# Attention of a gated block: attended context copied by ScalarE and multiplied by W1, with the bias added to x by Pool

## Chip, cores and metric

The kernel runs on one core of one Trainium2 chip. The metric is the device time of one execution in microseconds, here the median of three runs. Below, TensorE is PE, VectorE is DVE, ScalarE is ACT, and Pool is the GpSimd engine.

## What is computed

The input x has 4 batches of 1024 tokens with 256 features, the context 4 batches of 154 tokens. The reference, cut to what matters:

```python
h = layernorm(x)
Sim = (h @ w1)[:, :, None] + (c @ w2)[:, None, :] + einsum('bid,bjd->bij', h * w3, c) + b_sim
A = softmax(Sim, axis=2)
hq_hat = einsum('bij,bjd->bid', A, c)                    # attended context
Batt = softmax(max(Sim, axis=2), axis=1)
hc_hat = broadcast(einsum('bi,bid->bd', Batt, h))        # one row per batch
feats = concat([h, hq_hat, h * hq_hat, h * hc_hat])
x = x + tanh(g_xattn) * (feats @ W_qv + b_qv)
y = layernorm(x)
x = x + tanh(g_ffn) * ffn(y)     # gated, with 16-bit quantized activations and 4-bit weights
```

W_qv has four blocks of 256 rows, W0 to W3. W1 is the block that multiplies the attended context.

## The kernel before

The kernel has two stages. The first, up to about 216 us of the profiled execution, does the attention, the residual and the second layer norm; the second is the feed-forward part. Only the first is touched.

The first stage works on 16 units n of 256 tokens, four per batch, in one software-pipelined loop over steps m, written out by hand once for each engine (N = 16, NP = 4, LAG = 7; b, s = m // 4, m % 4). There is no planner: every engine runs its list in order, and semaphores tie the lists together. In step m:

- PE (L615 to L654): `project(m-7)`, `turn_h(m)` (transposes of the normed x), `score(m-1)`, `turn_a(m-2)` (transposes of the softmax), `attend(m-3)` (L499, weights of the softmax times context, into hq_bank), `turn_y(m-8)`. In steps with s = 3 the projection stands at the end instead ("late"), so that two projections follow each other: project(0) and project(1), project(4) and project(5), and so on. In steps with s = 2 the projection has row sums of the batch between its matmuls and waits first for an exponent (eb_rdy) of ScalarE.
- ACT (L855 on): `turned_h(m)`, `norm_x(m+1)`, `batch_exp` in steps with s = 1, `turned_a(m-2)`, `exps(m-1)`, `normed(m-1)` (scales the softmax, waits for DVE's reciprocal), `turned_y(m-8)`, `context_k`, and the weight conversion `weight_f`.
- DVE (L1207 on): `context_bias`, `residual(m-7)` (x + tanh(g) times the projection, and its statistics), `scored(m-1)`, `row_shift`, `batch_max`, `norm_x1(m-7)` (second layer norm, waits for Pool's power), `normed(m-1)` (the reciprocal, L1046), `attended(m-3)` (L1048, the product of hq_bank with hT), `max_y`, `stats(m+3)`, and in some steps work on the feed-forward weights: `weight_scales` in steps 8, 12, 16, `weight_unit` in 10, 14, 18, `weight_values` in 11, 15, 19.
- Pool (L401 on): `y_std(m-7)` and `row_std(m+3)`, powers of two elements; `weight_q` in steps 9, 10, 13, 14, 17, 18 and `weight_n` in 11, 15, 19. `row_std` ends with step 12.

For one unit, `project` (L510) sums into PSUM: the transposed softmax aT times cw, the product prT times W2, and hT times we, where we joins W0 and W3. The tile cw is the context times W1 plus the bias: PE multiplies it once per batch (`context_w`, L457, in step 1 and in every step with s = 0), and DVE adds the bias and stores it (`context_wv`, L1024, one step later). Two places wait for it: the first projection of a batch, and `batch_max` on PE (L562), which writes the same PSUM bank m_bank and waits with

```python
pe.wait_ge(cw_rdy, min(b + 2, B))
```

`attend(n)` writes hq_bank and waits for pr_rdy, that is for DVE's product of the unit before.

## Time and profile before

| | |
|---|---|
| median of 3 runs | 488.28 us (487.01 to 489.61) |
| profiled execution: time | 486.99 us |
| profiled execution: span | 485.2 us |
| mean granted clock of TensorE | 0.993 of full speed |
| PE busy | 461.5 us (95%) |
| DVE busy | 344.0 us (71%) |
| ACT busy | 266.7 us (55%) |
| Pool busy | 63.1 us (13%) |

The span reaches from the first to the last instruction of the core; the execution's own time has 1.8 us around it. Busy shares are means over both stages. The granted clock is what the chip allows TensorE at a time, as a share of 2.4 GHz; 0.50 is 1.2 GHz. A line number such as L1054 is a line of the kernel before; a number in brackets at the end of a timeline row is the idle time of that engine before the instruction, with what ended it.

### The profile page before, as it was taken

Reading aid. Unit: us, or ns where it says so; the run is one execution under the profiler, and the core shown is the slowest. Engines: PE = TensorE matmul, PEld = TensorE weight load, DVE = VectorE, ACT = ScalarE, POOL = GpSimd, SP = SyncE. Lnnn points to the kernel's source line nnn. Section 1 sums busy time; section 2 is a strip of 40 time slices with the busy share of each in tenths; the row PEclk is TensorE's granted clock in tenths of the full one; section 3 lists DMA queues with packets and bytes.
Section 4 is the critical chain, followed back from the end, with each engine's and each line's share of the span. In section 5 each row is a group of like instructions: output and inputs, shape, how many; then the busy total and the mean of one; then the engine's idle time right before and its main releaser. Section 6 shows DMA issues by size and latency. Waiting matters only on the chain.

```text
span 485.2 us, 6854 instructions
## 1 busy us (share of the span) xinstructions
PE 461.5 (95%) x2528; PEld 304.6 (63%) x2528; DVE 344.0 (71%) x649; ACT 266.7 (55%) x325; POOL 63.1 (13%) x61
## 2 busy tenths in 40 slices
PE   4899999998999997998999999999999999799997
PEld 3787884986578846783444444444444444588886
DVE  6455483859264935687644378999998888898874
ACT  3795142624241300426633459999567777888760
POOL 1111111213110311310000003343200000000000
PEclk9999999999899998999999999999999999999999
DMA  8930000200020002002000000000000000234442
GB/s 236 327 119 1 0 2 0 88 0 1 1 88 0 1 0 86 2 0 88 0 0 0 0 1 0 0 1 0 0 1 1 0 0 0 88 111 151 135 142 72
DMA packets 20673, 21.15 MB, mean 44 GB/s; under 512 B 825, under 2 KB 20392, under 8 KB 20648
## 3 DMA queue, kind: packets, MB, share of 16 engines
q1 hardware_dynamic: 20628, 20.82, 13.5%
q8 instruction: 15, 0.25, 0.2%
q14 instruction: 10, 0.08, 0.1%
q10 hardware_dynamic: 20, 0.00, 0.0%
HBM read 12.43 MB, written 8.39 MB: 43 GB/s over the span
## 4 chain that ended last, share of the span: by engine, by line
PE 68%; issue 15%; DVE 13%; ACT 2%; POOL 1%; DMA 1%; ACTq 0%; POOLq 0%; DVEq 0%
PE ps L676 17%; PE ps L711 11%; PE ps L681 9%; PE ps L527 4%; PE ps L506 4%; PE ps L531 4%; PE ps L523 4%; PE ps L569 3%; PE ps L486 3%; PE ps L472 1%; PE ps L495 1%; DVE st L1066 1%; PE ps L462 1%; DVE xa L1062 1%; DVE yb L1079 1%
## 5 line engine op out<-in xcount | busy, mean ns | idle before, releaser
L676 PE MATMUL ps<-xh,wuh 128*128 128x512 f16 x192 | 72.8, 379 | 0.1
L676 PE MATMUL ps<-xh,wul 128*128 128x512 f16 x192 | 72.8, 379 | 0.0
L681 PE MATMUL ps<-xl,wuh 128*128 128x512 f16 x192 | 57.1, 379 | 0.0
L1300 DVE TENSOR_REDUCE cols<-hid x10 | 22.9, 2286 | 24.7 <-ACT hid L891 24.7
L711 PE MATMUL ps<-wdl,oh 128*128 128x256 f16 x168 | 37.4, 273 | 0.0
L711 PE MATMUL ps<-wdh,oh 128*128 128x256 f16 x168 | 37.4, 273 | 0.0
L676 PE MATMUL ps<-xh,wgh 128*128 128x512 f16 x96 | 36.4, 379 | 0.7 <-DVE xh L1288 0.7
L676 PE MATMUL ps<-xh,wgl 128*128 128x512 f16 x96 | 36.4, 379 | 0.0
L527 PE MATMUL ps<-wv,prT 128*128 128x256 f32 x128 | 35.9, 396 | 0.0
L523 PE MATMUL ps<-cw,aT 77*128 77x256 f32 x128 | 34.7, 385 | 0.9 <-ACT cols L840 0.9
L783 ACT ACTIVATE hT<-ps 128x512 f32<-128x512 f32 x16 | 9.5, 591 | 46.6 <-PE ps L472 46.6
L531 PE MATMUL ps<-we,hT 128*128 128x256 f32 x128 | 34.4, 392 | 0.0
L891 ACT ACTIVATE hid<-ps 128x2048 f32 x10 | 18.8, 1875 | 27.9 <-PE ps L681 27.9
L676 PEld LDWEIGHTS ps<-xh,wuh 128*128 (+1 forms) x192 | 18.8, 98 | 23.1 <-issue 0.6
L681 PEld LDWEIGHTS ps<-xl,wuh 128*128 (+1 forms) x192 | 18.8, 98 | 22.7
L676 PEld LDWEIGHTS ps<-xh,wul 128*128 (+1 forms) x192 | 18.8, 98 | 22.5
L506 PE MATMUL ps<-aT,cx 77*128 77x256 f32 x128 | 31.2, 388 | 0.0
L1360 DVE TENSOR_TENSOR gq<-gq,ps 128x2048 bf16<-128x2048 int16 x11 | 25.1, 2285 | 6.0 <-ACT au L943 6.0
L973 ACT ACTIVATE oq<-hid,cols 128x1536 int16 (+1 forms) x15 | 23.6, 1571 | 10.2 <-DVE ol L1416 10.2
L1321 DVE TENSOR_REDUCE cols<-ps 128x1 f32<-128x2048 f32 x12 | 27.4, 2287 | 2.1 <-PE ps L681 2.1
L527 PEld LDWEIGHTS ps<-wv,prT 128*128 128x128 f32 x128 | 23.6, 192 | 8.2 <-issue 5.2
L681 PE MATMUL ps<-xl,wgh 128*128 128x512 f16 x96 | 28.6, 379 | 0.0
(211 smaller groups left out, 953.5 us busy)
## 6 DMA issues: line engine op xcount, KB each, us to landing
x_scratch<-xa SPq DMA_DIRECT2D x4, 1024.0 KB, 4.4
xo<-x_scratch SPq DMA_DIRECT2D x16, 256.0 KB, 2.7
out_dram<-xo SPq DMA_DIRECT2D x15, 256.0 KB, 2.1
xa<-in_x SPq DMA_DIRECT2D x3, 1024.0 KB, 12.6
xa<-in_x SPq DMA_DIRECT2D x4, 256.0 KB, 4.3
wv<-in_L_xattn_W_qv SPq DMA_DIRECT2D x1, 1024.0 KB, 8.6
wr<-in_L_ffn_w_gate SPq DMA_DIRECT2D x1, 768.0 KB, 9.5
wr<-in_L_ffn_w_up SPq DMA_DIRECT2D x1, 768.0 KB, 10.9
```

Of the source, the lines that this page charges most:

```text
L506: mm = pe.matmul(hq_bank[:, d * PT:(d + 1) * PT], cx[b][0:JP, k, d * P:(d + 1) * P], aT[0:JP, par, k, q], start=k == 0, stop=k == 1)
L523: pe.matmul(o_, aT[0:JP, par, k, q], cw[0:JP, b % 3, k, :], start=k == 0, stop=False)
L527: pe.matmul(o_, prT[:, par, d, q], wv[:, 2 * KD + d, :], start=False, stop=False)
L531: mm = pe.matmul(o_, hT[:, par, d, q], we[:, par, d, :], start=False, stop=d == KD - 1)
L676: pe.matmul(ps[hf][:, q, :], w_[:, d, ds(k * P, P)], xh[:, d, n], start=d == 0 and w_ is wh, stop=False)
L681: mm = pe.matmul(ps[hf][:, q, :], wh[:, d, ds(k * P, P)], xl[:, d, n], start=False, stop=d == KD - 1)
L711: mm = pe.matmul(down_ps(par)[:, t], o_[:, par, k, q], w_[:, k, :], start=not low and k == 0 and w_ is wdh, stop=low and k == KF - 1)
L891: act.activation(unit(hid, k, hf), ps_half(hf), ACT.Copy).then_inc(half_free[hf], 1)
L973: act.activation(oq[:, par], hid[:, :, ds(c * CD, CD)], ACT.Copy, scale=c_co).then_inc(oqa_rdy, 1)
L1300: dve.tensor_reduce(gmx[:, ds(k * 2 + hf, 1)], unit(hid, k, hf), AX.X, ALU.max, apply_absolute_value=True).then_inc(gm_done, 1)
L1321: dve.tensor_reduce(umx[:, u:u + 1], ps_half(u % 2), AX.X, ALU.max, apply_absolute_value=True).then_inc(half_free[u % 2], 1)
L1360: dve.tensor_tensor(g_.bitcast(BF16), g_, ps_half(hf), ALU.mult).then_inc(half_free[hf], 1)
```

## The change

PE no longer multiplies the context by W1. ScalarE copies the attended context of every unit from hq_bank to SBUF (hqT), and the projection takes hqT times W1 in place of aT times cw. DVE's product reads hqT instead of hq_bank. The bias, multiplied by tanh(g), is added to x by Pool (`bias_x`), and the residual waits for it. aT shrinks to a ring of three units.

```diff
--- before.py
+++ after.py
@@ -144,7 +144,7 @@
     a = copy_of(r_hid)
     xa = place(a, "xa", [P, B * TB, D], F32)
     hT = place(a, "hT", [P, 2, KD, S], F32)
-    aT = place(a, "aT", [JP, 2, 2, S], F32)
+    hqT = place(a, "hqT", [P, 2, KD, S], F32)
     prT = place(a, "prT", [P, 2, KD, S], F32)
     h = place(a, "h", [P, 2, TB, D], F32)
 
@@ -156,7 +156,7 @@
     cx01 = place(a, "cx01", [JP, 2, 2, D], F32)
     cx23 = place(copy_of(r_wg), "cx23", [JP, 2, 2, D], F32)
     cx = [cx01[:, 0], cx01[:, 1], cx23[:, 0], cx23[:, 1]]
-    cw = place(a, "cw", [JP, 3, 2, D], F32)
+    aT = place(a, "aT", [JP, 3, 2, PT], F32)
 
     a = copy_of(r_wd)
     cbi = place(a, "cbi", [P, 2, J], F32)
...
@@ -395,6 +395,14 @@
                 wm = wr[:, m, :].rearrange("p (n k) -> p n k", k=QB)
                 pool.tensor_tensor(wm, wm, wsc[:].unsqueeze(2).broadcast_to([P, NB, QB]), ALU.mult).then_inc(wn_rdy, 1)
 
+            def bias_x(n):
+
+                pool.wait_ge(h_rdy, n + 1)
+                if n == 0:
+                    pool.wait_ge(txb_rdy, 1)
+                x_ = xa[:, 2 * n:2 * n + 2, :]
+                pool.tensor_tensor(x_, x_, txb[:].unsqueeze(1).broadcast_to([P, 2, D]), ALU.add).then_inc(xb_rdy, 1)
+
             pool.wait_ge(mhalf_rdy, 1)
             for n in range(NP):
                 row_std(n)
@@ -403,6 +411,8 @@
                     y_std(m - LAG)
                 if 1 <= m and m + 3 < N:
                     row_std(m + 3)
+                if 4 <= m < N + 4:
+                    bias_x(m - 4)
                 for i in range(3):
                     if m in (W_AT[i] - 1, W_AT[i]):
                         weight_q(i, m - W_AT[i] + 1)
@@ -441,7 +451,7 @@
             def turn_context(b):
                 pe.wait_ge(cx_in[b], 16)
                 ge(pe, hc_rdy, b - 1)
-                ge(pe, cw_rdy, b)
+                ge(pe, cbi_rdy, b)
                 for k in range(2):
                     for d in range(KD):
                         tr = pe.transpose(m_bank[:, d * J + k * JP:d * J + (k + 1) * JP],
@@ -453,15 +463,6 @@
                 for d in range(KD):
                     mm = pe.matmul(m_bank[:, 0:J], w2b[:, d, :], cxT[:, d, :], start=(d == 0), stop=(d == KD - 1))
                 mm.then_inc(cbi_ps, 1)
-
-            def context_w(b):
-                pe.wait_ge(cbi_rdy, b + 1)
-                pe.wait_ge(wqv_in, 16)
-                for k in range(2):
-                    for d in range(KD):
-                        mm = pe.matmul(m_bank[0:JP, k * D:(k + 1) * D], cxT[:, d, k * JP:(k + 1) * JP], wv[:, KD + d, :],
-                                       start=(d == 0), stop=(d == KD - 1))
-                mm.then_inc(cw_ps, 1)
 
             def turn_h(n):
                 b, s, par = place_of(n)
@@ -499,12 +500,11 @@
             def attend(n):
                 b, s, par = place_of(n)
                 pe.wait_ge(aT_rdy, n + 1)
-                ge(pe, pr_rdy, n)
-                q = slice(s * PT, (s + 1) * PT)
+                ge(pe, hqT_rdy, n)
                 for d in range(KD):
                     for k in range(2):
                         mm = pe.matmul(hq_bank[:, d * PT:(d + 1) * PT], cx[b][0:JP, k, d * P:(d + 1) * P],
-                                       aT[0:JP, par, k, q], start=k == 0, stop=k == 1)
+                                       aT[0:JP, n % 3, k, :], start=k == 0, stop=k == 1)
                 mm.then_inc(hq_ps, 1)
 
             def project(n, summed=None):
@@ -512,17 +512,18 @@
                 if summed is not None:
                     pe.wait_ge(eb_rdy, summed + 1)
                 pe.wait_ge(pr_rdy, n + 1)
+                if n == 0:
+                    pe.wait_ge(wqv_in, 16)
                 if s == 0:
-                    pe.wait_ge(cw_rdy, b + 1)
                     pe.wait_ge(we_rdy, b + 1)
                 ge(pe, x1_rdy, n - 1)
                 for t in range(2):
                     q = slice(s * PT + t * P, s * PT + (t + 1) * P)
                     o_ = last_f(t) if n == L else f_bank[n % 2][:, t * D:(t + 1) * D]
-                    for k in range(2):
-                        pe.matmul(o_, aT[0:JP, par, k, q], cw[0:JP, b % 3, k, :], start=k == 0, stop=False)
+                    for d in range(KD):
+                        pe.matmul(o_, hqT[:, par, d, q], wv[:, KD + d, :], start=d == 0, stop=False)
                         if summed is not None:
-                            row_sum(summed, 4 * t + k)
+                            row_sum(summed, 4 * t + d)
                     for d in range(KD):
                         pe.matmul(o_, prT[:, par, d, q], wv[:, 2 * KD + d, :], start=False, stop=False)
                         if summed is not None:
@@ -561,7 +562,7 @@
 
             def batch_max(b):
                 pe.wait_ge(diag_rdy, b + 1)
-                pe.wait_ge(cw_rdy, min(b + 2, B))
+                pe.wait_ge(cbi_rdy, min(b + 2, B))
                 pe.matmul(m_bank[:, 0:P], ones[:], diag[:], start=True, stop=True).then_inc(m_ps, 1)
 
             def row_sum(b, t):
@@ -645,10 +646,6 @@
                     turn_y(m - LAG - 1)
                 if s == 3 and b + 1 < B:
                     context_bias(b + 1)
-                if m == 1:
-                    context_w(0)
-                if s == 0 and 1 <= b < B:
-                    context_w(b)
                 if LAG <= m and late:
                     project(m - LAG)
                 if N + 3 <= m < N + 6:
@@ -803,9 +800,16 @@
             def turned_a(n):
                 b, s, par = place_of(n)
                 act.wait_ge(at_ps, n + 1)
+                ge(act, hq_ps, n - 2)
+                act.activation(aT[0:JP, n % 3, :, :],
+                               a_bank[0:JP, :].rearrange("p (k n) -> p k n", k=2), ACT.Copy).then_inc(aT_rdy, 1)
+
+            def attended(n):
+                b, s, par = place_of(n)
+                act.wait_ge(hq_ps, n + 1)
                 ge(act, f_ps, n - 2 * NP + 1)
-                act.activation(aT[0:JP, par, :, s * PT:(s + 1) * PT],
-                               a_bank[0:JP, :].rearrange("p (k n) -> p k n", k=2), ACT.Copy).then_inc(aT_rdy, 1)
+                act.activation(hqT[:, par, :, s * PT:(s + 1) * PT], hq_bank.rearrange("p (d n) -> p d n", d=KD),
+                               ACT.Copy).then_inc(hqT_rdy, 1)
 
             def turned_y(n):
                 act.wait_ge(yT_ps, n + 1)
@@ -822,7 +826,7 @@
 
             def turned_context(b):
                 act.wait_ge(cxT_ps, b + 1)
-                ge(act, cw_ps, b)
+                ge(act, cbi_ps, b)
                 act.activation(cxT[:], m_bank[:, 0:2 * J].rearrange("p (d j) -> p d j", d=KD), ACT.Copy).then_inc(cxT_rdy, 1)
 
             def context_k(b):
@@ -869,6 +873,8 @@
                     normed(m - 1)
                 if s == 1 and b == 1:
                     batch_exp(b - 1)
+                if 3 <= m <= N + 2:
+                    attended(m - 3)
                 if LAG < m:
                     turned_y(m - LAG - 1)
                 if s == 3 and b + 1 < B:
@@ -1021,12 +1027,6 @@
                 dve.wait_ge(cbi_ps, b + 1)
                 dve.tensor_scalar(cbi[:, b % 2, :], m_bank[:, 0:J], c_bs, None, ALU.add).then_inc(cbi_rdy, 1)
 
-            def context_wv(b):
-                dve.wait_ge(cw_ps, b + 1)
-                ge(dve, f_ps, NP * (b - 2))
-                dve.tensor_tensor(cw[0:JP, b % 3], m_bank[0:JP, :].rearrange("p (k n) -> p k n", k=2),
-                                  bqb[0:JP, :].unsqueeze(1).broadcast_to([JP, 2, D]), ALU.add).then_inc(cw_rdy, 1)
-
             def scored(n):
                 b, s, par = place_of(n)
                 dve.wait_ge(sc_ps, n + 1)
@@ -1048,16 +1048,16 @@
             def attended(n):
                 b, s, par = place_of(n)
                 q = slice(s * PT, (s + 1) * PT)
-                dve.wait_ge(hq_ps, n + 1)
+                dve.wait_ge(hqT_rdy, n + 1)
                 dve.wait_ge(hT_rdy, n + 1)
                 ge(dve, f_ps, n - 2 * NP + 1)
-                dve.tensor_tensor(prT[:, par, :, q], hq_bank.rearrange("p (d n) -> p d n", d=KD), hT[:, par, :, q],
-                                  ALU.mult).then_inc(pr_rdy, 1)
+                dve.tensor_tensor(prT[:, par, :, q], hqT[:, par, :, q], hT[:, par, :, q], ALU.mult).then_inc(pr_rdy, 1)
 
             def residual(n):
 
                 g = 2 * n
                 dve.wait_ge(f_ps, n + 1)
+                dve.wait_ge(xb_rdy, n + 1)
                 x_ = xa[:, g:g + 2, :]
                 dve.scalar_tensor_tensor(x_, f_bank[n % 2].rearrange("p (t d) -> p t d", t=2), c_tx, x_,
                                          ALU.mult, ALU.add).then_inc(x1_rdy, 1)
@@ -1082,6 +1082,7 @@
 
             def last_y():
 
+                dve.wait_ge(xb_rdy, N)
                 for t in range(2):
                     x_ = xa[:, 2 * L + t, :]
                     dve.wait_ge(l_f_ps, t + 1)
@@ -1128,6 +1129,8 @@
                 dve.tensor_scalar(c_hc, m_bank[:, HC:HC + KD], c_rs, None, ALU.mult).then_inc(hc_rdy, 1)
                 dve.wait_ge(hc_rdy, b + 1)
                 ge(dve, f_ps, NP * (b - 1))
+                if b == 0:
+                    dve.wait_ge(wqv_in, 16)
                 for d in range(KD):
                     i_ = dve.scalar_tensor_tensor(we[:, b % 2, d, :], wv[:, 3 * KD + d, :], c_hc[:, d:d + 1], wv[:, d, :],
                                                   ALU.mult, ALU.add)
@@ -1198,21 +1201,16 @@
             dve.wait_ge(x0_in[2], 16)
             stats(2)
             row_shift(1)
-            dve.tensor_copy(bqb[:], f_bank[1][:, 0:D]).then_inc(bqb_rdy, 1)
             dve.wait_ge(x0_in[3], 16)
             stats(3)
             row_shift(2)
-            dve.wait_ge(bqb_rdy, 1)
             dve.wait_ge(tanh_rdy, 1)
+            dve.tensor_scalar(txb[:], f_bank[1][:, 0:D], c_tx, None, ALU.mult).then_inc(txb_rdy, 1)
             for m in range(N + LAG - 1):
                 b, s = m // NP, m % NP
                 late = s == 3
                 if m == 0:
                     row_shift(3)
-                if m == 2:
-                    context_wv(0)
-                if s == 1 and 1 <= b < B:
-                    context_wv(b)
                 if s == 0 and 1 <= b < B:
                     context_bias(b)
                 if s == 2 and 1 < b <= B:
```

On DVE, steps 12 and 13, from the product of unit 9 to the residual of unit 6. Before:

```order
L1054 TENSOR_TENSOR prT<-ps,hT 128x2x256
L1106 TENSOR_REDUCE cols<-yb 128x1
L1004 BN_STATS st<-xa 128x6 x2
L1007 BN_AGGR cols<-st 128x2 x2
L1011 TENSOR_SCALAR cols<-cols 128x2
L1146 TENSOR_REDUCE wsc<-wr 128x48
L1148 TENSOR_SCALAR wsc<-wsc 128x48
L1149 TENSOR_REDUCE cols<-wsc 128x1
L1150 TENSOR_SCALAR wdiag<-ident,cols 128x128
L1151 RECIPROCAL wri<-wsc 128x48
L1027 TENSOR_TENSOR cw<-ps,bqb 77x512
L1062 SCALAR_TENSOR_TENSOR xa<-ps,cols,xa 128x512
```

And with the change:

```order
L1054 TENSOR_TENSOR prT<-hqT,hT 128x2x256
L1107 TENSOR_REDUCE cols<-yb 128x1
L1010 BN_STATS st<-xa 128x6 x2
L1013 BN_AGGR cols<-st 128x2 x2
L1017 TENSOR_SCALAR cols<-cols 128x2
L1149 TENSOR_REDUCE wsc<-wr 128x48
L1151 TENSOR_SCALAR wsc<-wsc 128x48
L1152 TENSOR_REDUCE cols<-wsc 128x1
L1153 TENSOR_SCALAR wdiag<-ident,cols 128x128
L1154 RECIPROCAL wri<-wsc 128x48
L1062 SCALAR_TENSOR_TENSOR xa<-ps,cols,xa 128x512
```

The addition that made cw has gone, and the product reads hqT (SBUF) instead of PSUM; the order is otherwise the same.

On ACT, from turned_a to context_k in step 11, with the change (before, the row of hqT isn't there):

```order
L804 ACTIVATE aT<-ps 77x512
L788 ACTIVATE sc,cols<-sc,cols 128x154 x2
L797 ACTIVATE sc<-sc,cols 128x154 x2
L811 ACTIVATE hqT<-ps 128x2x256
L816 ACTIVATE yT<-ps 128x2x256
L836 ACTIVATE cp<-cxT,wcol 128x154 x2
```

The copy to hqT stands behind the exponentials and the scaling (L797) of a unit two later.

On Pool, from y_std(5) in step 12 to weight_n in step 15, with the change (L377 is y_std, L373 row_std, L404 bias_x, L390 and L396 weight_q and weight_n):

```order
L377 TENSOR_TENSOR cols<-cols 128x2
L373 TENSOR_TENSOR cols<-cols 128x2
L404 TENSOR_TENSOR xa<-xa,txb 128x512
L377 TENSOR_TENSOR cols<-cols 128x2
L404 TENSOR_TENSOR xa<-xa,txb 128x512
L390 TENSOR_TENSOR wr<-wr,wri 128x768
L377 TENSOR_TENSOR cols<-cols 128x2
L404 TENSOR_TENSOR xa<-xa,txb 128x512
L390 TENSOR_TENSOR wr<-wr,wri 128x768
L377 TENSOR_TENSOR cols<-cols 128x2
L404 TENSOR_TENSOR xa<-xa,txb 128x512
L396 TENSOR_TENSOR wr<-wr,wsc 128x1536
```

In step 12 bias_x stands behind row_std; from step 13 on it stands directly behind y_std and ahead of the weight instruction.

## Rows read from the trace of the kernel before

**Rows 1.** Busy us by stretch: PE, PEld, DVE, ACT, POOL, then PEclk, DMA share, GB/s.
```profile
24.00:36.00 12.00, 12.00 (x74) 10.52 (x73) 7.01 (x34) 11.05 (x33) 1.88 (x3) 1.00 0.37 128
...
108.00:120.00 12.00, 9.95 (x53) 8.22 (x52) 11.65 (x31) 4.94 (x12) 4.15 (x3) 1.00 0.00 1
```
**Rows 2.** Groups by line, first stage: busy us, mean ns | idle before.
```profile
L1106 DVE TENSOR_REDUCE cols<-yb 128x1 f32<-128x512 f32 x15 | 10.2, 679 | 0.2
L783 ACT ACTIVATE hT<-ps 128x512 f32<-128x512 f32 x16 | 9.5, 591 | 46.6 <-PE ps L472 46.6
```
**Rows 3.** Timeline, steps 12 to 14: start us, duration us, engine, line, operation.
```profile
113.35 0.67 DVE L1054 TENSOR_TENSOR prT<-ps,hT 128x512 f32<-128x512 f32 x1
...
114.11 0.57 ACT L812 ACTIVATE yT<-ps 128x512 f32<-128x512 f32 x1
...
118.48 0.62 DVE L1027 TENSOR_TENSOR cw<-ps,bqb 77x512 f32<-77x512 f32 x1
119.02 0.73 DVE L1062 SCALAR_TENSOR_TENSOR xa<-ps,cols,xa 128x512 f32<-128x512 f32 x1
119.25 0.46 PE L565 MATMUL ps<-diag,ones 128*128 128x128 f32 x2 [2.06 <-DVE cw L1027]
...
120.94 0.28 DVE L1118 TENSOR_REDUCE cols<-ps 128x1 f32<-128x128 f32 x1
...
125.31 0.60 PE L523 MATMUL ps<-cw,aT 77*128 77x256 f32 x2
```
**Rows 4.** Timeline, from the batch reduction of step 17 to project(11).
```profile
169.00 0.28 DVE L1118 TENSOR_REDUCE cols<-ps 128x1 f32<-128x128 f32 x1
...
169.76 0.70 PE L523 MATMUL ps<-cw,aT 77*128 77x256 f32 x2 [0.92 <-ACT cols L840]
```
**Rows 5.** Stretches of 1 us behind two waits; PEclk is third from the end.
```profile
121.00:122.00 1.00, 1.00 (x6) 0.99 (x5) 0.39 (x3) 1.00 (x4) 0.89 (x2) 0.50 0.00 0
...
189.00:190.00 1.00, 1.00 (x4) 0.82 (x3) 0.00 (x0) 0.00 (x0) 0.00 (x0) 0.50 0.00 0
```
**Rows 6.** Timeline, three other waits of TensorE (steps 15, 19 and 20).
```profile
143.97 0.66 PE L495 MATMUL ps<-ident,sc 128*77 128x128 f32 x4 [0.79 <-ACT sc L800]
...
187.28 0.66 PE L542 MATMUL ps<-ident,yb 128*128 128x128 f32 x4 [2.97 <-DVE yb L1079]
...
202.87 1.76 PE L600 MATMUL ps<-ident,wr 128*128 128x128 f32 x12 [1.13 <-DVE wgl L1172]
```
**Rows 7.** Timeline of TensorE: context_w(2) in step 8, then step 9 to project(3).
```profile
63.15 1.89 PE L462 MATMUL ps<-wv,cxT 128*77 128x256 f32 x8
...
64.88 1.03 PE L523 MATMUL ps<-cw,aT 77*128 77x256 f32 x4
...
70.06 0.39 PE L565 MATMUL ps<-diag,ones 128*128 128x128 f32 x2
...
74.38 0.60 PE L523 MATMUL ps<-cw,aT 77*128 77x256 f32 x2
```
**Rows 8.** Timeline of the start: the first exponent and the first row sums.
```profile
35.96 0.28 ACT L840 ACTIVATE cols<-cols 128x8 f32<-128x8 f32 x1
...
37.26 3.62 PE L569 MATMUL ps<-h,cols 128*1 128x256 f32 x16
```
**Rows 9.** Timeline, Pool and VectorE side by side in steps 16 and 17; last, all of L1079: min/median/max ns.
```profile
158.76 2.77 POOL L396 TENSOR_TENSOR wr<-wr,wsc 128x1536 f32<-128x1536 f32 x1 [3.95 <-ACT wr L844]
...
159.06 2.50 DVE L1073 TENSOR_SCALAR cols<-cols 128x2 f32<-128x2 f32 x1
...
169.16 0.69 POOL L377 TENSOR_TENSOR cols<-cols 128x2 f32<-128x2 f32 x1 [6.84 <-DVE cols L1073]
...
169.81 1.48 POOL L390 TENSOR_TENSOR wr<-wr,wri 128x768 f32<-128x768 f32 x1
169.89 1.88 DVE L1079 TENSOR_SCALAR yb<-xa,cols 128x256 f32<-128x256 f32 x2 [0.61 <-POOL cols L377]
...
L1079 DVE TENSOR_SCALAR yb<-xa,cols x30: 400/408/1554, 56.9 to 213.0; 128x256 f32<-128x256 f32 x30
```

More of the change, by code:

```diff
@@ L167, in build @@
     wrow = place(a, "wrow", [3 * KD, P], F32)
-    bqb = place(a, "bqb", [P, D], F32)
+    txb = place(a, "txb", [P, D], F32)
     hrow = place(copy_of(r_wu), "hrow", [1, D], F32)
```

8 lines of the change are left out of this document (4 added, 4 removed).

## The prediction, made before the changed kernel was run

> **What bounds the kernel now.** I read the stretches first [rows 1]. The change lies in the first stage, up to about 216 us. In the start ScalarE is nearly full (11.05 of 12 us). Later TensorE is busy nearly all the time; where it falls short (9.95 of 12 us from 108 to 120), VectorE is at 11.65. So TensorE sets the pace in most steps and VectorE in a few. The groups by line give durations [rows 2]; then I read the timeline at the gaps.
>
> Step m means pass m of the main loop; n is a unit of 256 tokens, projected at step n+7. Where two projections stand back to back, VectorE catches up. In steps 12/13 and 16/17 it doesn't: behind the product it runs weight_scales, the residual and the batch maximum, and the next projection with row sums waits for all of it through ScalarE's exponent. At step 13 TensorE waits 2.06 us at L565 for cw, which VectorE built just before [rows 3]; before project(11) it waits 0.92 us for the exponent [rows 4].
>
> **TensorE's clock.** After the 2.06 us wait the granted clock goes to 0.50, that is 1.2 instead of 2.4 GHz, and it does so after the 2.97 us wait at 187.28 [rows 5, 6]. The waits of 0.92 and 0.79 us are followed by no such stretch. The price: from L565 to the projection the same work takes 74.38 − 70.06 = 4.32 us at step 9 [rows 7] and 125.31 − 119.25 = 6.06 us at step 13 [rows 3], so 1.74 us for a fall.
>
> **What is removed.** context_w runs four times.
> - Step 8: 64.88 − 63.15 = 1.73 us of TensorE [rows 7], taken whole: TensorE then reaches project(3) at 74.38 − 1.73 = 72.65, and VectorE, which loses context_wv there and gains the wait described below, has the exponent ready at about 72.7. **−1.73**.
> - Step 12: the same 1.73 us, the 2.06 us wait, and its fall of the clock, 1.74: 5.53 us. TensorE would reach project(7) at 125.31 − 5.53 = 119.78 [rows 3]. What is late next is the exponent, see below.
> - Steps 1 and 4 lie in the start, under ScalarE's work; without that cover they would bring 1.7 us each.
>
> **What is added: a handover.** ScalarE copies the attended context: 16 copies at 0.59 us [rows 2], 9.5 us in all. By itself that costs little, since ScalarE is mostly idle after step 7. What counts is the place. VectorE's product of unit m−3 now needs a copy that stands in ScalarE's queue behind normed(m−1), which itself waits for the reciprocal directly in front of that product. At step 12 the product started at 113.35. ScalarE is through with normed at 114.11, where turned_y starts; the copy takes 0.59, the hop 0.05: 114.75, **1.40 us later** [rows 3]. Behind it on VectorE stand max_y, the statistics, weight_scales. Where TensorE has 10 us of projections ahead, this is hidden; where VectorE sets the pace, it is not.
> - Step 12/13: the residual comes at 119.02 + 1.40 − 0.54 (context_wv gone, start to start) = 119.88. To the batch reduction it is 120.94 − 119.02 = 1.92 us [rows 3], from there to TensorE's restart 0.76 [rows 4]: 122.6. TensorE is there at 119.78 and waits 2.8 us. I take a new fall of the clock, since 2.06 us was enough: it gains 125.31 − 122.6 − 1.74, **−1.0**. So of 5.5 us removed one is left.
> - Step 16/17: the same 1.40 us, with no context_wv to set against it: **+1.40**.
> - Start, steps 3 to 5: exponentials, normed, copy, product, statistics and scores now form one ring over two engines. Copy and product together add up to 1.2 us a step, 3.6 in three; against that go a ScalarE wait behind context_w(0), 0.5 us, the slack of either engine, and the exponent's head start on the row sums (35.96 against 37.26) [rows 8]. Bounds −0.5 (the slack takes all) and +1.5; I take **+0.15**, near the lower, as both engines still wait in every one of these steps now.
>
> **What is added: the bias on Pool.** 16 adds of 512 elements. Pool takes 2.77 us for 1536 elements and 1.48 for 768 [rows 9]: 1.69 ns an element, 1.05 us for 512 (ends: 0.69 for its two-element instruction, 1.48 for 768). They are ready three steps before the residual. What isn't covered is who is kept out: beside Pool's L396 a two-element TENSOR_SCALAR of VectorE takes 2.50 us, and norm_x1 (L1079) takes 1.88 beside L390 [rows 9], where 0.73 is usual for two of about 0.41. From step 13 on Pool has no row_std, so bias_x follows y_std at once, and norm_x1 waits for the same y_std. Pool's next instruction starts 0.65 us after y_std, VectorE's 0.73; VectorE is let go some 0.15 us before Pool's end (159.06 + 2.50 − 0.17 against 158.76 + 2.77): 0.65 + 1.05 − 0.15 − 0.73 = 0.8, taken as **0.75 us a meeting**.
> - Steps 15 and 16, norm_x1(8) and (9), both on the way to the exponent before project(11): **+1.5**. With the handover that wait is 0.92 + 1.40 + 1.5 = 3.8 us, so the clock falls: **+1.74**.
> - Step 14: bias_x(10) pushes weight_q behind it, and both keep out L1132 and the small instructions after it, on the way to turn_a(13), which waits 0.79 us already [rows 6]. Between +0.3 (VectorE gets in between the two) and +1.25 (it doesn't): **+0.7**.
> - Step 18, the same before the 2.97 us wait, with L1132 starting ahead of Pool: bounds +0.2 and +1.2, **+0.4**.
> - Step 19: norm_x1(12) delays the weight values and so turn_w(1), which waits 1.13 us already [rows 6]: **+0.75**.
>
> The Trainium skill's "GPSIMD Engine Reference" (section "Elementwise — side-by-side cycle accounting") has a two-input add at 1.96 times VectorE's; on this trace's 0.67 us for the product that is an estimate of 1.3 us. By it each meeting costs 0.3 us more and the sum 0.9 more; no run here shows it yet.
>
> The product now reads two SBUF tensors instead of one and PSUM. VectorE's 512-element reduction from SBUF takes 0.679 us [rows 2], the product from PSUM 0.67 [rows 3]: no difference taken. The Trainium skill's "VectorE: DVE Perf Modes" (section on the TRN2 errata) charges PSUM 62 cycles more, an estimate of 0.06 us; by it steps 12 and 16 would each get that back. The projection's matmuls keep their 256 columns, so I take nothing for them.
>
> **Sum.** −1.73 − 1.0 + 1.40 + 0.15 + 1.5 + 1.74 + 0.7 + 0.4 + 0.75 = +3.9 us. On the profiled execution's 486.99 that is 490.9. The median of the runs, 488.28, lies 1.3 above it, so I predict **492.2**.
>
> **Rivals.** About 0.5% (2.4 us) is what a measurement of this kernel can tell from no change.
> - *The clock stays up and Pool's adds slip past* (faster). For it: 0.92 us cost no clock, and Pool's and VectorE's starts are only 0.08 us apart, so VectorE may come first. Then −1.73 − 2.7 + 1.40 + 0.15 = −2.9: **485.4**. It decides before project(7) and project(11): waits of 2.8 and 2.3 us must leave the clock at 1.00. Against it: 2.06 us didn't. Chance 0.15.
> - *Handover only*: Pool's adds miss VectorE, the clock falls twice. −1.73 − 1.0 + 1.40 + 1.74 + 0.15 = +0.6: **488.9**. Chance 0.24.
> - *Pool's queue becomes the bound*: weight_q takes its place right behind bias_x in steps 14 and 18 (+0.55, +0.8), and the wait before turn_a(13) grows to 2 us, so the clock falls there too (+1.74): **495.3**. Chance 0.14.
> - The forecast, itself 490 to 494: 0.47.
>
> **Numbers.** Range 486.0 to 495.5: all but the better part of the first rival and the tail of the third, under 2 in 10 together. Slower by over 0.5% (above 490.7), most of the forecast and the third: 0.54. Faster (below 485.8): 0.14. The same: 0.32.
>
> **What would show it.** A product 1.3 to 1.5 us after its reciprocal in steps 12 and 16; 1.4 to 1.6 us for the two norm_x1 instructions from step 13 on, beside a Pool instruction of 1.05 us; TensorE waiting 2.8 us before project(7) and 3.8 before project(11), each followed by a stretch at 0.50; no wait at L565. It is wrong if TensorE's wait before project(11) stays under 2 us, if norm_x1 keeps its 0.73, or if Pool's add takes much more than 1.5 us.

## The result, and the profile after

| | before | changed |
|---|---|---|
| median | 488.94 us | 499.04 us |
| range | 487.01 to 490.62 (4 runs) | 495.89 to 500.75 (4 runs) |
| profiled execution | 486.99 us | 498.97 us |
| its span | 485.2 us | 497.1 us |
| mean granted clock | 0.993 | 0.976 |

The change makes the kernel slower: 1.020 times the time of before, with a 95% interval of 1.016 to 1.024, some 10 us. I had forecast 492.2, with 486.0 to 495.5 as the range. The sign was right, the size was not.

The head of the page of the changed kernel, and then the shares of its chain that ended last:

```profile
PE 462.5 (93%) x2496; PEld 302.4 (61%) x2496; DVE 352.9 (71%) x645; ACT 274.6 (55%) x341; POOL 81.6 (16%) x77
...
PE   4789999997989697898999999999999999899997
...
PEclk9999999999899887989999999999999999899999
...
PE 50%; DVE 20%; issue 19%; ACT 8%; POOL 1%; DMA 0%; ACTq 0%; POOLq 0%; DVEq 0%
```

TensorE has about as much busy time as before (462.5 us against 461.5), though context_w is gone and 32 matmuls with it. So the busy time is not what the 12 us of the span are made of in any simple way: part of the work simply ran at a lower clock. The clock's row has five 8s and one 7 (a slice is 12.4 us); three of these lie side by side, from 161 to 199 us. On the chain TensorE has 50%, before it had 68%. That row prices nothing by itself: in e3 below, which is faster than before, it is 46%.

The four large waits of TensorE in the first stage, and the one before turn_a(13), from the timeline of the changed kernel (start us, us, engine, line, operation, tiles, and in brackets the idle time before and who ended it):

```profile
122.52 0.70 PE L524 MATMUL ps<-wv,hqT 128*128 128x256 f32 x2 [3.03 <-ACT cols L844]
...
143.86 0.66 PE L496 MATMUL ps<-ident,sc 128*77 128x128 f32 x4 [0.96 <-ACT sc L797]
...
173.27 1.22 PE L524 MATMUL ps<-wv,hqT 128*128 128x256 f32 x2 [4.09 <-ACT cols L844]
...
193.19 1.11 PE L543 MATMUL ps<-ident,yb 128*128 128x128 f32 x4 [3.23 <-DVE yb L1079]
...
210.65 1.86 PE L601 MATMUL ps<-ident,wr 128*128 128x128 f32 x12 [2.08 <-DVE wgl L1175]
```

The first stands where before had 2.06 us at the batch maximum [rows 3]. The third is the 0.92 us before project(11) [rows 4], now 4.09. The others are those of [rows 6]: 0.79, 2.97 and 1.13 us, now 0.96, 3.23 and 2.08. And what the clock did around them (stretch, its length, busy us and count of PE, PEld, DVE, ACT, POOL, then the granted clock, DMA share, GB/s):

```profile
120.00:122.00 2.00, 0.00 (x0) 0.00 (x0) 1.90 (x9) 0.00 (x0) 0.07 (x1) 1.00 0.00 0
122.00:127.00 5.00, 4.48 (x10) 1.47 (x10) 3.68 (x10) 3.08 (x11) 3.35 (x3) 0.66 0.01 2
171.00:173.00 2.00, 0.00 (x0) 0.00 (x0) 1.68 (x7) 0.18 (x1) 0.33 (x1) 0.55 0.00 0
173.00:178.00 5.00, 4.73 (x9) 1.67 (x10) 4.03 (x4) 1.66 (x5) 3.09 (x3) 0.50 0.02 3
...
191.00:193.00 2.00, 0.00 (x0) 0.00 (x0) 1.86 (x7) 0.00 (x0) 1.33 (x1) 0.67 0.21 70
193.00:198.00 5.00, 4.80 (x14) 3.96 (x15) 1.34 (x3) 0.60 (x1) 0.00 (x0) 0.50 0.00 2
210.00:212.00 2.00, 1.35 (x10) 1.09 (x11) 2.00 (x4) 1.93 (x5) 2.00 (x1) 1.00 0.00 0
212.00:216.00 4.00, 4.00 (x14) 3.29 (x13) 3.05 (x10) 1.04 (x2) 0.85 (x2) 0.57 0.02 4
430.00:435.00 5.00, 5.00 (x33) 3.77 (x32) 3.80 (x6) 5.00 (x5) 0.00 (x0) 0.66 0.27 94
```

A stretch's length times (1 − clock) is the clock lost in it. 122 to 127 lost 5 × 0.34 = 1.7 us, 212 to 216 and 430 to 435 the same. 171 to 178 lost 0.9 + 2.5 = 3.4, twice as much in one piece, and 191 to 199 again 3.4. Over the whole span the mean clock gives the total: 0.024 × 497.1 = 11.9 us, against 0.007 × 485.2 = 3.4 before. I call 1.7 us of lost clock **one fall**; before had two, the changed kernel has seven. What was lost inside the wait itself can cost nothing, since TensorE did nothing there: up to the two restarts that is 1.0 us of the third place (from 171.2 to 173.27) and 0.8 of the fourth.

These counts are of the two profiled executions. By their mean clocks the four runs of the changed kernel lost 8.4 to 13.5 us, about five to eight falls; the 26 runs of before that stand beside e1 lost about one to three (0.996 to 0.989).

The same landmarks of TensorE in the two timelines give a ledger. The forecast's column adds up its own terms in their order.

| reached by TensorE | before | changed | shift | forecast |
|---|---|---|---|---|
| turn_h in step 8 | 59.05 | 60.22 | +1.17 | +0.15 |
| turn_h in step 9 | 70.28 | 69.72 | −0.56 | −1.58 |
| turn_a(13) | 143.97 | 143.86 | −0.11 | −1.88 |
| project(11) | 169.76 | 173.27 | +3.51 | +1.02 |
| turn_y(11) | 187.28 | 193.19 | +5.91 | +3.16 |
| turn_w(1) | 202.87 | 210.65 | +7.78 | +3.91 |
| first matmul of stage two | 225.24 | 234.70 | +9.46 | +3.91 |
| end of the span | 485.2 | 497.1 | +11.9 | +3.9 |

### The profile page after: what moved, and what is told of

Its sections match the earlier page's. It is cut to its first block, busy times and chain, and to the rows that moved or that the text cites. A ratio compares the mean times of both kernels' runs of the same rounds, so it can differ in the third digit from the quotient of the medians.

```text
span 497.1 us, 6840 instructions
## 1 busy us (share of the span) xinstructions
PE 462.5 (93%) x2496; PEld 302.4 (61%) x2496; DVE 352.9 (71%) x645; ACT 274.6 (55%) x341; POOL 81.6 (16%) x77
## 3 DMA queue, kind: packets, MB, share of 16 engines
q1 hardware_dynamic: 20628, 20.82, 13.3%
## 4 chain that ended last, share of the span: by engine, by line
PE 50%; DVE 20%; issue 19%; ACT 8%; POOL 1%; DMA 0%; ACTq 0%; POOLq 0%; DVEq 0%
PE ps L708 11%; PE ps L673 8%; PE ps L524 5%; PE ps L528 4%; PE ps L678 4%; DVE cols L1319 4%; PE ps L532 4%; PE ps L570 4%; PE ps L506 3%; DVE hid L1335 2%; PE ps L487 2%; ACT hid L920 2%; DVE yb L1079 1%; DVE st L1066 1%; DVE xa L1062 1%
## 5 line engine op out<-in xcount | busy, mean ns | idle before, releaser
L524 PE MATMUL ps<-wv,hqT 128*128 128x256 f32 x128 | 38.1, 415 | 7.1 <-ACT cols L844 7.1
L528 PE MATMUL ps<-wv,prT 128*128 128x256 f32 x128 | 37.4, 410 | 0.0
L524 PEld LDWEIGHTS ps<-wv,hqT 128*128 128x128 f32 x128 | 24.5, 204 | 13.5 <-ACT cols L844 7.6
L528 PEld LDWEIGHTS ps<-wv,prT 128*128 128x128 f32 x128 | 24.9, 202 | 9.3 <-issue 6.1
L1335 DVE CUSTOM_DVE_ANT_0 hid<-ag,sq 128x2048 f32<-128x2048 int16 x12 | 29.1, 2424 | 0.2
## 6 DMA issues: line engine op xcount, KB each, us to landing
xa<-in_x SPq DMA_DIRECT2D x3, 1024.0 KB, 12.4
```

Source lines behind the costliest of these rows:

```text
L524: pe.matmul(o_, hqT[:, par, d, q], wv[:, KD + d, :], start=d == 0, stop=False)
L528: pe.matmul(o_, prT[:, par, d, q], wv[:, 2 * KD + d, :], start=False, stop=False)
L1335: dve.tensor_tensor_reduce(half_of(hid, u), ag[:, u % 2, :], sq[u % 2][:], 1.0, 0.0, ALU.mult, ALU.max, pmx[:, u:u + 1]).then_inc(p_rdy, 1)
```

## The experiments

Each kernel ran 4 to 10 times, beside runs of before on the same chip (medians 488.75 to 489.13 us). "Lost" is the clock lost in the profiled execution, added up over stretches of 1 us.

| | median us | ratio to before, 95% | lost us |
|---|---|---|---|
| changed kernel | 499.04 | 1.020 [1.016, 1.024] | 11.9 |
| bias later (e1) | 490.85 | 1.004 [1.000, 1.008] | 6.8 |
| product from PSUM (e2) | 492.58 | 1.008 [1.005, 1.010] | 10.2 |
| both (e3) | 485.77 | 0.995 [0.993, 0.998] | 3.4 |
| bias add left out (e8) | 491.63 | 1.005 [1.002, 1.008] | 6.8 |
| waits filled (e4) | 491.78 | 1.007 [1.004, 1.010] | 1.7 |
| one wait filled (e12) | 497.22 | 1.016 [1.013, 1.020] | 8.5 |
| before, waits filled (e7) | 486.12 | 0.995 [0.992, 0.997] | 1.7 |
| product last, bias later (e6) | 482.97 | 0.989 [0.985, 0.993] | 3.4 |
| e6, filled (e10) | 480.64 | 0.984 [0.981, 0.987] | 0.0 |
| e3, copy later, filled (e9) | 480.76 | 0.984 [0.981, 0.986] | 0.0 |

### The bias behind norm_x1

```
                 if 4 <= m < N + 4:
+                    if 13 <= m:
+                        pool.wait_ge(y_rdy, m - LAG + 1)
                     bias_x(m - 4)
```

> From step 13 on Pool's add waits until norm_x1 of the same step is done, so the two no longer meet. Theory A (handover, Pool's meetings and clock falls add up, a fall of 3.4 us behind a wait of over 3 us): the wait before project(11) goes from 4.09 to about 1.9 us, turn_w(1)'s from 2.08 to about 1.1; with the clock that comes back the time falls from 499.0 by 6 to 9 us, to 490 to 493. Theory B (the handover alone makes the loss, Pool's adds are incidental): 497 to 499. Theory C (Pool's queue is what matters, later adds push weight_q further): 499 or more.

Measured 490.85 us, 8.2 under the changed kernel, as expected. Two waits were not: I expected about 1.9 us before project(11) and 1.1 before turn_w(1). TensorE's waits in its timeline:

```profile
124.67 0.86 PE L526 MATMUL ps<-wv,hqT 128*128 128x256 f32 x2 [3.01 <-ACT cols L846]
...
144.37 0.66 PE L498 MATMUL ps<-ident,sc 128*77 128x128 f32 x4 [0.22 <-ACT sc L799]
...
172.29 0.70 PE L526 MATMUL ps<-wv,hqT 128*128 128x256 f32 x2 [2.92 <-ACT cols L846]
...
190.06 1.12 PE L545 MATMUL ps<-ident,yb 128*128 128x128 f32 x4 [1.73 <-DVE yb L1081]
...
206.15 1.76 PE L603 MATMUL ps<-ident,wr 128*128 128x128 f32 x12 [1.73 <-DVE wgl L1177]
```

The wait before project(7) stays at 3.0 us, so moving Pool's add does nothing there. Before project(11) it goes from 4.09 to 2.92, so the edit brings 1.2 us there; without any add (e8, below) the wait is 2.33, and what the other 0.6 is made of was not traced. Before turn_a(13) it goes to 0.22, less than before's 0.79 [rows 6], and before turn_y(11) to 1.73 against 2.97. The reason is weight_q, which stands behind the add and now starts later too. In before it runs beside VectorE's two instructions that make `we` for the next batch, in the changed kernel the add does and then weight_q, and in e1 neither. Step 14, of before, the changed kernel and e1:

```profile
139.91 1.46 DVE L1132 SCALAR_TENSOR_TENSOR we<-wv,cols 128x256 f32<-128x256 f32 x2
```

```profile
138.77 2.49 DVE L1135 SCALAR_TENSOR_TENSOR we<-wv,cols 128x256 f32<-128x256 f32 x2
```

```profile
140.89 0.88 DVE L1137 SCALAR_TENSOR_TENSOR we<-wv,cols 128x256 f32<-128x256 f32 x2
```

In step 18 the three take 2.13, 1.94 and 0.88 us. So part of e1's gain is a delay of weight_q, which has nothing to do with the bias. The rest of the 8.2 us is clock: three falls fewer in the profiled execution, 5.1 us.

### The product straight from PSUM

VectorE reads hq_bank as before the change, ScalarE copies when VectorE is done, and the projection waits for the copy.

```
-                dve.wait_ge(hqT_rdy, n + 1)
+                dve.wait_ge(hq_ps, n + 1)
...
-                dve.tensor_tensor(prT[:, par, :, q], hqT[:, par, :, q], hT[:, par, :, q], ALU.mult)
+                dve.tensor_tensor(prT[:, par, :, q], hq_bank.rearrange("p (d n) -> p d n", d=KD), hT[:, par, :, q], ALU.mult)
...
-                act.wait_ge(hq_ps, n + 1)
+                act.wait_ge(pr_rdy, n + 1)
...
-                pe.wait_ge(pr_rdy, n + 1)
+                pe.wait_ge(hqT_rdy, n + 1)
```

> VectorE's product reads PSUM again, as before, and ScalarE copies the attended context behind it; Pool's adds stay. Theory A: VectorE no longer waits 1.28 us for the copy; the waits before project(7) and project(11) shrink by 1.4 us each, to 1.6 and 2.7 us, and one or two quanta of clock (1.7 us each) come back: 492 to 495. Theory B (the handover makes the whole loss): 484 to 488, below the kernel before. Theory C (Pool makes the whole loss): 498 to 500.

Measured 492.58 us, 6.5 under the changed kernel.

```profile
118.87 0.70 PE L524 MATMUL ps<-wv,hqT 128*128 128x256 f32 x2 [1.62 <-ACT cols L844]
...
166.66 1.22 PE L524 MATMUL ps<-wv,hqT 128*128 128x256 f32 x2 [2.70 <-ACT cols L844]
...
189.06 1.09 PE L543 MATMUL ps<-ident,yb 128*128 128x128 f32 x4 [5.04 <-ACT yT L816]
```

Both waits for the exponent are 1.4 us shorter than in the changed kernel (3.03 to 1.62, 4.09 to 2.70): that is the handover as forecast, 1.40, at both places. The edit also made a wait of its own. ScalarE's copy at 187.83 stands in its queue ahead of turned_y and now waits for the product, which stands behind norm_x1 on VectorE; so TensorE waited 5.04 us for yT at 189.06. The clock lost 3.4 us around the 2.70 (166 to 173) and 3.4 around the 5.04 (186 to 194), 1.2 of it inside that wait.

### Both together

> Both edits together: product from PSUM with the copy behind it, and Pool's adds behind norm_x1. Theory A: what is left is the removal of context_w and context_wv against 16 copies and adds that nothing waits for; wait before project(7) about 1.6 us, before project(11) about 0.9, clock falls as in the kernel before or one fewer: 482 to 486, under the 488.9 of before. Rival (the matmuls on 128 rows, or the copies themselves, cost something in every step): 488 to 492.

Measured 485.77 us. With both costs out, the change's idea is a little faster than before: ratio 0.995 with an interval of 0.993 to 0.998. The waits are 1.63, 1.54, 3.53 (the new wait for yT) and 1.73 us, and only around the 3.53 was clock lost, 3.4 us. The two costs together are 13.3 us of time. Alone they bring 8.2 and 6.5, sum 14.7, so they are nearly independent. I had expected a wait of about 0.9 us before project(11); it was 1.54. And not all of the gain over before is the change's: in e3 too the two instructions for `we` take 0.88 us, where before has 1.46 and 2.13.

### No bias add at all

The kernel leaves out Pool's adds and the waits on them, so that the output lacks the bias.

> The changed kernel with the addition of the bias on Pool left out, so the output lacks the bias; the handover through ScalarE stays. Theory A: as with the later adds (490.9), and less, since weight_q and weight_n come 1.3 us earlier and L1135 is held once only: 488 to 491, with a wait before project(11) of about 2.3 us (0.92 + 1.40). Rival (even the later adds cost nothing): 490.5 to 491.5. If the handover were free: 484.

```profile
123.89 0.70 PE L522 MATMUL ps<-wv,hqT 128*128 128x256 f32 x2 [2.70 <-ACT cols L842]
...
171.53 0.70 PE L522 MATMUL ps<-wv,hqT 128*128 128x256 f32 x2 [2.33 <-ACT cols L842]
...
190.58 1.12 PE L541 MATMUL ps<-ident,yb 128*128 128x128 f32 x4 [2.98 <-DVE yb L1076]
...
205.92 1.76 PE L599 MATMUL ps<-ident,wr 128*128 128x128 f32 x12 [1.13 <-DVE wgl L1171]
```

Measured 491.63 us: the handover alone costs 2.5 us net of the gain of context_w. The wait before project(11) is 2.33 us, 0.01 from 0.92 + 1.40, and turn_y(11) and turn_w(1) wait as long as before (2.98 and 1.13). This is my second rival, "handover only", for which I had worked out 488.9. Its waits come out and its time is 2.7 us above it: there were four falls where that sum had three (1.7 us). The fourth came at 46 us, behind a wait of 0.98 us that the sum didn't have (see the start, below). And e8 is level with e1, so an add placed behind norm_x1 costs nothing that can be seen in the median: it lengthens two waits by 0.6 us each and shortens turn_y(11)'s by 1.25, by the delay of weight_q.

### Filling TensorE's waits

Matmuls whose result nobody reads (the projection that follows starts its sums anew over them) are put into the queue ahead of the waiting instruction: 6 before project(7), 9 before project(11), 7 before turn_y(11), 4 before turn_w(1), of 256 columns each. They only keep TensorE at work.

```
+            def fill(n, k):
+                pe.wait_ge(x1_rdy, n - 1)
+                for i in range(k):
+                    pe.matmul(f_bank[n % 2][:, 0:D], ident[:], wv[:, 0, :], start=True, stop=True)
...
+                if m in {14: 6, 18: 9}:
+                    fill(m - LAG, {14: 6, 18: 9}[m])
```

> The changed kernel with TensorE kept busy in its four long waits by matmuls that nobody reads: 6 before project(7), 9 before project(11), 7 before turn_y(11), 4 before turn_w(1). Nothing else moves. Theory A (the waits cost clock, 1.7 us of it for 2 to 3 us and 3.4 us for longer): the 10.2 us of clock lost in the first stage come back, except what the fillers overrun; 489 to 492, with the granted clock at 1.00 there. Rival (the low clock is there for another reason, or costs nothing since other engines set the pace): 497 to 500.

Measured 491.78 us, 7.3 under the changed kernel, with VectorE, ScalarE and Pool as they were there. The clock lost 1.7 us instead of 11.9, in one fall at 45 us that no filling matmul was near. That is what the waits' clock costs the changed kernel, not yet its share of the change's 10 us, since before loses clock in its waits as well.

The same was done to the kernel before, with 4 such matmuls ahead of the batch maximum of step 13 and 6 ahead of turn_y(11):

> The kernel before, with its two long waits filled by matmuls that nobody reads: 4 at the batch maximum of step 13 (2.06 us), 6 before turn_y(11) (2.97 us). Theory A: the clock no longer falls there and 2 x 1.7 us come back: 485.0 to 486.0 against 488.7. Rival (the fall at step 13 is hidden by VectorE, which sets the pace there): 486.5 to 487.5, only the second comes back. If neither counts: 488 to 489.

486.12 us, 3.0 under before, just above the 485.0 to 486.0 expected. Both falls of the first stage are gone, and one came at 415 us, in stage two. With the waits of both kernels filled, 491.78 stands against 486.12: 5.7 of the 10.1 us between the medians remain, and 4.4 are clock. By the spans (489.1 against 483.5) it is 5.6 and 6.3 of 11.9. Without its clock, before has a span of 485.2 − 3.4 = 481.8; this kernel's is 483.5 − 1.7 = 481.8. So the filling matmuls cost nothing that can be seen here.

Then the changed kernel with the 9 before project(11) alone:

> The changed kernel with fillers before project(11) only (9, in the wait of 4.09 us). Theory A (the clock lost behind this one wait is 3.4 us, and all of it is time): 495 to 496, with the granted clock at 1.00 from 171 to 179 us. If a fall costs 1.7 us however long the wait, as the prediction took it: 497 to 498. If nothing comes back: 499.

```profile
170.00:178.00 8.00, 7.79 (x35) 4.77 (x33) 7.17 (x15) 1.84 (x5) 3.42 (x3) 1.00 0.01 2
190.00:196.00 6.00, 3.59 (x11) 3.08 (x12) 3.42 (x10) 0.60 (x1) 1.54 (x1) 0.72 0.11 37
```

From 170 to 178 us the clock stays at 1.00, where the changed kernel was at 0.50. The median is 497.22, 1.8 us lower, and the span 1.8 lower. That is the time of the expectation's rival, in which a fall costs 1.7 us however long the wait. But behind that wait 2.4 us of clock had been lost. Two other places differ: a fall came at 45 to 50 us, which the changed kernel's profile doesn't have, after the same wait of 0.98; and behind turn_y(11)'s wait, 3.23 us in both, the clock lost 6 × 0.28 = 1.7 us instead of the 2.7 that lay behind it in the changed kernel. −2.4 + 1.7 − 1.0 = −1.7, near to the −1.8 measured. Whether filling one wait moved the other falls or they differ from execution to execution, this pair of profiles can't tell; the same wait of 0.98 us had a fall behind it in e1, e4, e8 and e11 too.

### What Pool's add costs

In one run the add's second operand was changed so that it stands still: each of 16 columns of the bias is added to 32 columns of x (the output has a wrong bias for it).

> The changed kernel with 16 columns of the bias tile, each repeated 32 times, added in place of all 256 twice, so the output has a wrong bias; Pool's add has as many elements as in the change, but its second operand stands still for 32 elements at a time, as in weight_q. If the estimate of the prediction failed because weight_q's second operand stands still (1.69 ns an element), the add takes about 1.05 us in place of 1.27. If two-input work on Pool costs the same whatever the operand: 1.27.

The group of Pool's adds, of the changed kernel and then of this one (count, busy us, mean ns, idle before):

```profile
L404 POOL TENSOR_TENSOR xa<-xa,txb 128x512 f32<-128x512 f32 x16 | 20.3, 1268 | 0.0
```

```profile
L404 POOL TENSOR_TENSOR xa<-xa,txb 128x512 f32<-128x512 f32 x16 | 16.8, 1047 | 0.0
```

With the standing operand it takes 1.047 us, and my 1.05 was right for that kind. I had read 1.69 ns an element from weight_q [rows 9], whose scale is one number for 32 elements, and carried it over to an add whose bias moves at every element. The single run took 497.81 us. The two instructions that the add held in steps 15 and 16 took 1.45 and 1.18 us, 0.2 less each, and the wait before project(11) went from 4.09 to 3.96.

### A better place for the product

If ScalarE's copy comes late, VectorE can do its other work first. In e6 VectorE's product stands at the end of the step, and the bias behind norm_x1:

```
-                if 3 <= m <= N + 2:
-                    attended(m - 3)
                 if LAG <= m and late:
                     residual(m - LAG)
...
                 if N + 3 <= m < N + 6:
                     weight_parts(m - N - 3)
+                if 3 <= m <= N + 2:
+                    attended(m - 3)
```

> Product from hqT as in the change, but as VectorE's last work of a step, behind the statistics and the weight work; Pool's adds behind norm_x1. Theory A: the copy is then always there in time, the 1.28 us waits of VectorE vanish, and the product itself (0.6 us) leaves the way to the exponent too: wait before project(7) about 1.0 us, before project(11) about 0.9; 483 to 486, as good as the product from PSUM or better. Rival (a product at the end delays the scores of the next step in the start and gives the gain back): 487 to 490.

482.97 us, 1.1% under before. VectorE's wait at the product goes from 18.3 us in 14 waits to 2.1 in all. TensorE's four waits are 1.73, 1.63, 1.73 and 1.72 us; I had expected about 1.0 and 0.9 for the first two. All three engines do the change's work, and the span without lost clock is 481.2 − 3.4 = 477.8, 4.0 under that of before. Not all of the 4.0 need be the change's. The waits before turn_a(13) and turn_y(11) are 0.22 and 1.73 us, 1.8 less together than in before, and in e1, which has the same two, this came from weight_q starting later. The kernel before with weight_q moved back, and nothing else, was not run, so how much of the gain it would reach alone is open.

Two kernels put the parts together. e10 is e6 with 2, 2, 5 and 3 filling matmuls:

> Product from hqT as VectorE's last work of a step, Pool's adds behind norm_x1 (483.0 without fillers, 3.4 us of clock lost in its profiled run, 1.7 of it in the first stage), with fillers: 2 before project(7), 2 before project(11), 5 before turn_y(11), 3 before turn_w(1). If the clock is the only thing fillers bring: 480.5 to 481.5, level with the 480.8 of the version that multiplies from PSUM. If the 5 fillers overrun the 1.73 us wait before turn_y(11): 482 to 483.

e9 is e3 with ScalarE's copy moved behind turned_y, so that yT is not late, and 3, 3, 5 and 3 of them:

> Product from PSUM, ScalarE's copy behind it and behind turned_y, Pool's adds behind norm_x1, and fillers: 3 before project(7), 3 before project(11), 5 before turn_y(11), 3 before turn_w(1). The version without fillers took 485.8 with 3.4 us of clock lost in the profiled run. Theory A: all of it comes back and turn_y(11) waits 1 to 1.5 us less: 481 to 483. Rival (the fillers overrun the waits and cost what they save): 485 to 486.

480.64 us, as expected, and 480.76, just below what was; both are 1.6% under before and level with each other. The clock's row of e10 shows no slice below 9, and from 119 us on (e9's timeline) TensorE's waits at the old places are under half a microsecond:

```profile
PEclk9999999999999999999999999999999999999999
```

```profile
119.82 0.70 PE L526 MATMUL ps<-wv,hqT 128*128 128x256 f32 x2 [0.36 <-ACT cols L858]
...
165.02 0.70 PE L526 MATMUL ps<-wv,hqT 128*128 128x256 f32 x2 [0.24 <-ACT cols L858]
...
196.00 1.76 PE L609 MATMUL ps<-ident,wr 128*128 128x128 f32 x12 [0.42 <-DVE wgl L1189]
```

## Why the prediction was wrong in size and right in sign

**The step that failed is the term of the clock**: "1.74 for a fall", taken at most once per wait, and with one added fall in the sum. The profiled execution has five more falls than before, not one. Of its 11.9 us of lost clock 1.8 lie inside waits; the 10.1 behind them, against 3.4 before, are 6.7 us more, where the sum had 1.74. That is 5.0 of the 8.0 us by which the span missed. The other 3.0 are mostly the start (1.0), stage two beside its fall (0.7), and 0.3 each in steps 9 to 12, in step 14 and before project(11). The price of one fall was right (1.71 measured); how many there would be was not. The median missed by 6.8: the 1.3 us that the sum put on top of the profiled execution was before's, and the changed kernel's median lies 0.1 above its own.
- Before project(11) I had a wait of 3.8 us and one fall. It was 4.09, the clock was already at 0.55 in the last 2 us of the wait, and 2.4 us were lost behind it.
- Behind turn_y(11) I kept before's one fall, since the wait only grew from 2.97 to 3.23 us. It became two, 2.7 us behind the wait.
- Behind turn_w(1) I had none. The wait had been 1.13 us, and the sum itself makes it 1.9. Measured 2.08, as long as the 2.06 of [rows 3] that I had read as "enough". The row to see this was in my own text; the sum added 0.75 us for the wait and stopped.
- Stage two: behind a wait of 2.44 us the clock fell at 430. Before had the same wait, 2.43, without a fall. No term of the change leads there, and e7, whose stage two is before's, has a fall there as well. So this one isn't shown to be the change's; without it the profiled executions differ by four falls.

e4 and e7 bear the size out: filling gives back 7.3 us in the changed kernel and 3.0 in before, so a little over 4 us of the difference is clock, where the sum had 1.74. None of my signs of being wrong watched the number of falls, and none came true outright: norm_x1 kept its 0.72 us in step 16, but another instruction was held in its place.

**Step by step, the rest.**
- *context_w in step 8, −1.73:* from turn_h in step 8 to turn_h in step 9 the shift went from +1.17 to −0.56, so −1.73. Right.
- *Start, +0.15:* measured +1.17, within the bounds of −0.5 and +1.5 but at the wrong end. The row sums start at 37.52 instead of 37.26 [rows 8], and 0.20 of that stands already at the first turn_h (10.69 instead of 10.49). The rest is a wait I had not looked at: turn_context waits for VectorE's first column product, L1129, which stands behind the product of the attended context.

```profile
44.65 0.69 DVE L1054 TENSOR_TENSOR prT<-hqT,hT 128x512 f32<-128x512 f32 x1 [1.28 <-ACT hqT L811]
...
45.46 0.22 DVE L1129 TENSOR_SCALAR cols<-ps,cols 128x2 f32<-128x2 f32 x1
```

```profile
45.78 0.46 PE L457 MATMUL ps<-ident,cx 77*128 77x77 f32 x4 [0.98 <-issue]
```

  The profile calls it "issue", but it ends 0.1 us after L1129, and before it was not there (that transpose started at 44.60). The handover's 1.3 us came through a second door; in e2 and e3, where the product doesn't wait for the copy, this wait is gone. Of the six profiled kernels that have it, all but the changed one had a fall behind it. Pool's adds meet VectorE in the start too, which the prediction had only from step 13 on: behind row_std stands bias_x, and VectorE's own instruction on row_std's result takes 1.22 us where before has 0.16.

```profile
48.49 1.27 POOL L404 TENSOR_TENSOR xa<-xa,txb 128x512 f32<-128x512 f32 x1
48.56 1.22 DVE L1024 SCALAR_TENSOR_TENSOR cols<-cols 128x2 f32<-128x2 f32 x1 [0.30 <-POOL cols L373]
```

  From the first turn_h to the row sums e8, without adds, takes 26.4 us, the changed kernel 26.8, e2 25.8.
- *The handover, 1.40:* right. VectorE waits 1.28 us for the copy. The group of waits (us in total, times, longest us), and the row at step 12:

```profile
DVE prT L1054 <- ACT hqT L811: 18.3, 14, 1.6
```

```profile
114.61 0.69 DVE L1054 TENSOR_TENSOR prT<-hqT,hT 128x512 f32<-128x512 f32 x1 [1.28 <-ACT hqT L811]
```

  It was forecast at 114.75. e2 and e8 give 1.4 us at both exponents.
- *Steps 12 and 13, −1.0:* TensorE's restart was forecast at 122.6 and came at 122.52, the wait at 2.8 and was 3.03, one fall behind it, none at the batch maximum. From step 12's turn_h (106.02, now 105.74) to step 14's (136.26, now 135.12) the shift moves by −0.86.
- *Step 14, +0.7:* +1.03, within its bounds. Most of it stands one instruction group earlier than I had it: the scores at 141.61 wait 0.62 us for VectorE's L1159, and turn_a(13) itself 0.96 instead of 0.79.
- *Two meetings in steps 15 and 16, 0.75 each:* the place was right in step 15, the price not. Pool's add and VectorE's norm_x1, of the changed kernel:

```profile
154.90 1.67 DVE L1079 TENSOR_SCALAR yb<-xa,cols 128x256 f32<-128x256 f32 x2 [0.82 <-POOL cols L377]
...
163.25 1.41 DVE L1115 TENSOR_SCALAR diag<-ident,cols 128x128 f32<-128x128 f32 x1
```

```profile
154.83 1.27 POOL L404 TENSOR_TENSOR xa<-xa,txb 128x512 f32<-128x512 f32 x1
...
163.30 1.27 POOL L404 TENSOR_TENSOR xa<-xa,txb 128x512 f32<-128x512 f32 x1
```

  The two norm_x1 instructions took 1.67 us instead of 0.73, so 0.94. In step 16 VectorE was ahead of Pool by one instruction and it was the diagonal, L1115, that took 1.41 us instead of 0.29. TensorE's wait was 4.09 us for my 3.8. Without any add it is 2.33 (e8), so the meetings cost 1.76 of it, where the sum had 1.5; the two held instructions alone would make 2.06.
- *Pool's add, 1.05 us:* 1.268. The Trainium skill's "GPSIMD Engine Reference" (section "Elementwise — side-by-side cycle accounting") has a two-input add at 1.96 times VectorE's, from which the prediction made an estimate of 1.3 us, and the trace agrees with it. By it the sum would have been 0.9 us higher, 493.1: nearer, and still inside my range, not the result.
- *The product from SBUF, nothing:* 0.691 us, and 0.680 from PSUM in e2. The Trainium skill's "VectorE: DVE Perf Modes" (section on the TRN2 errata) charges an operand in PSUM 62 cycles more, by which the product would be an estimated 0.06 us shorter from SBUF; here it was 0.01 longer, so the trace doesn't agree.
- *Step 19, +0.75:* turn_w(1) waited 2.08 us; I had 1.9.

So four of the waits of TensorE came out within 0.3 us of the sum's, and step 14's delay too, though at another place; the start didn't, and the clock behind the waits didn't. The rival in which the clock stays up was wrong altogether. The one that puts Pool's queue before turn_a(13) was wrong as well: the wait there is 0.96 us, not 2.

**What stays open.** Stage two is 262.4 us long, and was 260.0 before. 1.7 of that is the fall at 430. The other 0.7 stands in one wait of TensorE, for VectorE's gq:

```profile
370.52 0.39 PE L673 MATMUL ps<-xh,wuh 128*128 128x512 f16 x1 [0.81 <-DVE gq L1358]
```

Before has 0.1 us in all on that line, but e7, with the same code in stage two, waits 0.80 there and has 262.4 us with its own fall. So neither part of stage two is shown to come from the change. Some 0.3 us between steps 9 and 12 were not traced either. And I can't say beforehand whether a wait of 2 to 3 us costs one fall or two (the last section).

## What to carry to other kernels

An operation that moves to an idle engine costs its place in that engine's queue: here a copy of 0.57 us made VectorE wait 1.3 us fourteen times, because it stood behind work that needed VectorE's own result of a moment ago. Move the consumer back at the same time (e6), not only the copy over. When a sum ends in "TensorE now waits 2 or 4 us here", price each such wait again with its clock, also those that merely grew past what already cost one elsewhere in the trace. Price the waits of the kernel before in the same way. And try matmuls without a reader in it: ten of them brought 3 us in the kernel before, 26 brought 7 in the changed one.
